# Cross-attention in a decoder block: K, V and maxima units dealt evenly over twelve key steps, and the value product cut 112 + 112

## The chip, the cores and the metric

The kernel runs on one core of a Trainium2 chip. The metric is the device time of one execution in microseconds (us); the times shown are medians over runs.

## The reference

One decoder layer with post-norm, batch 32, 56 queries of width 128, and a context of 1500 rows of width 128 for each batch:

```
x = LN(x + linear_attention(x))                        # 16 heads of 8, 32 features
q = x @ Wq.T + bq;  k = ctx @ Wk.T + bk;  v = ctx @ Wv.T + bv
a = softmax(q k / sqrt(8)) v     per head              # 56 x 1500 scores, 16 heads
x = LN(x + a @ Wo.T + bo)
h = x @ W1 + b1
x = LN(x + relu(h + c1 * sin(theta + 0.1 h)) @ W2 + b2)
```

The cross-attention (second line to fourth) is most of the work and all of what the change touches.

## The kernel before, in words

The front part computes the linear attention for all batches and the queries of the cross-attention. Then comes one `body(b)` for each of the 32 batches, on each engine in its own written order: bodies 0 and 1, a loop over pairs of bodies, and bodies 30 and 31. A body has twelve key steps t of 125 context rows. The last part is the feed-forward network.

In a step TensorE makes the scores of all heads (`score`, L831, four matmuls of 224 columns, in two alternating pairs of PSUM banks), ScalarE takes their exponential (`exp`, L576), and TensorE multiplies the exponentials of the step before by the values (`pv`, L846 and L851) into bank 7, `O`. The value product has for each of four head groups one matmul over three of the group's four heads (168 columns, 32 weights: a block of ones for the denominators and the values) and one over the fourth (56 columns, 16 weights). They are fp32, and each leaves two records.

Between these, TensorE works on the batches that follow, in units. Each unit fills one of the three ring banks (banks 4 to 6), in turn:

- K (three a batch, L794): a third of the key projection, nine fp16 matmuls of 500 columns for three units, for batch b + 2. ScalarE rounds the result to fp16 (`k_hi`, L594, `kh`), and VectorE then writes the remainder (`k_lo`, L1091, `kl`), after which the bank is free.
- V (three a batch, L800): twelve matmuls of 128 columns for batch b + 1; ScalarE copies them to `v_ext` (L581).
- M (21 a batch, L807): scores over 500 keys whose maximum VectorE takes (`m_max`, L1098). After the 21st, `m_row` folds them, X (L811) transposes them, ScalarE copies that to `mT` and SyncE places it as row 96 of `q_diag`, so that the scores come out reduced by a bound on the maximum.
- R (L814, L815): spreads the denominators of batch b - 1; VectorE inverts them (L1112, `r_sb`) and scales O with them (L1116).
- Y (L820, in bodies of even b): the output projection of the pair of batches before.

Before a unit starts, TensorE waits until the unit that last held the bank is done (`held`, `DONE`). `unit_plan` places them: R at step 0, V after steps 0, 2 and 4, two or three M in each of steps 1 to 9, Y at step 6, X at step 11, and the three K units after step 11, with the last value product among them. VectorE takes the results in the same order; after the first K it copies O out of its bank (`o_copy`, L1126), which the next batch's first value product waits for.

`kh` and `kl` have one buffer each. SyncE copies them to `k_stack` by twelve transfers a batch (L355, two of three parts from `kh`). GpSimd splits the context into two fp16 halves (`split`, L442, L444) and makes the masked queries `q_diag` and `q_max`.

## Time and profile before

| | |
|---|---|
| median of 3 runs | 889.09 us (886.41 to 890.37) |
| the profiled execution, its time | 889.02 us |
| its span | 887.2 us |
| TensorE busy | 825.6 us, 93% of the span |
| VectorE busy | 692.8 us, 78% |
| ScalarE busy | 559.0 us, 63% |
| GpSimd busy | 294.3 us, 33% |
| mean granted TensorE clock | 0.974 |

The busy shares are of the whole span. A group of instructions is given by its line, engine and operation with its count and mean duration. The loop over the pairs fills most of the span; in the timeline a row is a run of like instructions, with the start of the first and the time they cover, and the distance between the starts of two rows is what the first really took. In the forty slices each digit is a share in tenths. A released wait is shown in brackets behind the row that had to wait.

### The profile page before, as it was taken

To read this page: it belongs to the slowest core of one execution; us is meant where nothing else is said; L and a number is where in the kernel's file an instruction comes from. 1 tells how busy PE (TensorE), PEld (TensorE's weight loads), DVE (VectorE), ACT (ScalarE), POOL (GpSimd) and SP (SyncE) were. 2 spreads that over 40 slices of the span, in tenths; PEclk is the share of its full clock that TensorE was granted. 3 is DMA by queue.
4 is the path that set the end of the run, shared out by engine and by line. 5 is a ranking of instruction groups with operands and counts; after the bars stand their busy time and mean duration, and the time that the engine had idled before them with its cause. 6 is when DMAs were issued, how large, how long until landed. Compare 5 with 4: busy or idle time off the path is not lost.

```text
span 887.2 us, 28853 instructions
## 1 busy us (share of the span) xinstructions
PE 825.6 (93%) x11074; PEld 534.8 (60%) x11074; DVE 692.8 (78%) x1245; ACT 559.0 (63%) x759; POOL 294.3 (33%) x170
## 2 busy tenths in 40 slices
PE   6788669999999999999999999999999999998884
PEld 3555426666666666666666666666666666666553
DVE  7767687778787878787878787878787878788498
ACT  4566517666666666666666666666666666666863
POOL 6010524333333333333333333333333333300263
PEclk9989959999999999999999999999999999999898
DMA  6000044333333333333333333333333332222001
GB/s 201 1 10 21 21 129 105 92 86 90 86 87 87 86 88 87 87 86 88 85 87 88 86 86 88 87 87 89 85 92 82 93 84 78 52 53 55 1 1 42
DMA packets 29864, 67.37 MB, mean 76 GB/s; under 512 B 8072, under 2 KB 13192, under 8 KB 29704
## 3 DMA queue, kind: packets, MB, share of 16 engines
q1 hardware_dynamic: 29832, 66.94, 28.7%
q8 instruction: 21, 0.34, 0.2%
q14 instruction: 11, 0.09, 0.0%
HBM read 27.50 MB, written 0.92 MB: 32 GB/s over the span
## 4 chain that ended last, share of the span: by engine, by line
PE 73%; DVE 15%; ACT 5%; issue 5%; DMA 1%; DVEq 0%; POOL 0%; ACTq 0%
PE psum L807 19%; PE psum L846 16%; PE psum L831 14%; PE psum L800 6%; PE psum L794 6%; DVE r_sb L1112 5%; PE psum L851 4%; ACT kh L594 2%; PE psum L722 2%; DVE kl L1091 2%; PE psum L820 2%; PE psum L708 1%; DVE k_stack L1226 1%; DVE rden L1025 1%; DVE mx L1098 1%
## 5 line engine op out<-in xcount | busy, mean ns | idle before, releaser
L1098 DVE TENSOR_REDUCE mx<-psum 128x1 f32<-128x500 f32 x672 | 413.0, 672 | 52.7 <-PE psum L807 49.5
L576 ACT ACTIVATE probs<-psum 125x896 f32<-125x896 f32 x384 | 352.7, 919 | 149.9 <-PE psum L831 146.4
L807 PE MATMUL psum<-kh,q_max 128*128 128x500 f16 x672 | 234.5, 383 | 7.3 <-DVE mx L1098 2.0
L831 PE MATMUL psum<-q_diag,k_stack 97*128 97x224 f16 x1536 | 212.9, 261 | 2.7 <-DMA q_diag<-mT 1.8
L846 PE MATMUL psum<-probs,v_ext 125*32 125x168 f32 x3072 | 189.3, 319 | 1.2 <-ACT probs L576 1.2
L831 PEld LDWEIGHTS psum<-q_diag,k_stack 97*128 97x128 f16 x1536 | 140.7, 98 | 46.6 <-issue 16.9
L442 POOL CAST c_hl<-c_in 128x1500 f16<-128x1500 f32 x32 | 45.9, 1434 | 267.8 <-PE psum L800 261.9
L1091 DVE SCALAR_TENSOR_TENSOR kl<-psum,pack,kh 128x500 f16<-128x500 f32 x96 | 68.0, 735 | 83.4 <-ACT kh L594 83.4
L846 PEld LDWEIGHTS psum<-probs,v_ext 125*32 125x32 f32 x3072 | 60.6, 108 | 114.9 <-issue 97.2
L450 POOL TENSOR_TENSOR q_diag<-q_stack,pack 96x896 f16<-96x896 f32 (+1 forms) x32 | 54.2, 1693 | 171.0 <-PE psum L831 158.7
L851 PE MATMUL psum<-probs,v_ext 125*16 125x56 f32 x3072 | 108.4, 213 | 0.0
L851 PEld LDWEIGHTS psum<-probs,v_ext 125*16 125x16 f32 x3072 | 90.0, 97 | 14.9
L444 POOL TENSOR_TENSOR c_hl<-c_in,c_hl 128x1500 f16<-128x1500 f32 x32 | 97.1, 3034 | 2.6
L581 ACT COPY v_ext<-psum 125x512 f32<-125x512 f32 x96 | 56.3, 586 | 60.2 <-PE psum L800 60.0
L807 PEld LDWEIGHTS psum<-kh,q_max 128*128 128x128 f16 x672 | 65.2, 97 | 47.8 <-DVE mx L1098 18.1
L594 ACT ACTIVATE kh<-psum,pack 128x500 f16<-128x500 f32 x96 | 63.6, 677 | 28.7 <-PE psum L794 28.7
L800 PE MATMUL psum<-WvH,c_hl 128*128 128x128 f16 x768 | 75.7, 221 | 0.0
L800 PE MATMUL psum<-WvL,c_hl 128*128 128x128 f16 x384 | 69.4, 219 | 0.0
L800 PEld LDWEIGHTS psum<-WvH,c_hl 128*128 128x128 f16 x768 | 55.8, 98 | 6.7
L794 PE MATMUL psum<-c_hl,WkH 128*128 128x500 f16 x192 | 58.6, 388 | 0.0
L459 POOL TENSOR_TENSOR q_max<-qh,pack 128x896 f16<-128x896 f32 (+1 forms) x32 | 54.0, 1688 | 0.0
L1112 DVE RECIPROCAL r_sb<-psum 128x224 f32<-128x224 f32 x32 | 49.5, 1547 | 0.2 <-PE psum L815 0.2
(143 smaller groups left out, 735.0 us busy)
## 6 DMA issues: line engine op xcount, KB each, us to landing
c_in<-ctx_in SPq DMA_DIRECT2D x32, 750.0 KB, 4.3
k_stack<-kh SPq DMA_DIRECT2D x256, 93.8 KB, 2.2
k_stack<-kl SPq DMA_DIRECT2D x128, 93.8 KB, 2.2
pack<-pack_in SPq DMA_DIRECT2D x1, 1107.0 KB, 5.9
q_stack<-qh SPq DMA_DIRECT2D x32, 32.0 KB, 1.8
out<-x_all SPq DMA_DIRECT2D x8, 112.0 KB
pack<-pack_in SPq DMA_DIRECT2D x1, 848.5 KB, 4.7
x_all<-x_in SPq DMA_DIRECT2D x2, 336.0 KB
```

Source lines behind the costliest of these rows:

```text
L444: nc.gpsimd.tensor_tensor(c_hl[:, buf, 1, 0:S], c_in[:, buf, :], c_hl[:, buf, 0, 0:S], ALU.subtract).then_inc(c_split, 1)
L576: nc.scalar.activation(probs[0:KP, t % PBUF, :].rearrange("p (a c) -> p a c", a=2), scores[t % 2][0:KP, :, 0:2 * GC], ACT.Exp, scale=SCALE ...
L594: nc.scalar.activation(kh[:, i * CH:(i + 1) * CH], bank[:, 0:CH], ACT.Identity, bias=w("bk")).then_inc(kh_done, 1)
L794: last = nc.tensor.matmul(bank[:, 0:CH], wt[:, :], c_hl[:, u, part, i * CH:(i + 1) * CH], start=(k == 0), stop=(k == 2))
L800: last = nc.tensor.matmul(bank[:, j * P:(j + 1) * P], c_hl[:, u, part, at:at + P], wt[:, :], start=(k == 0), stop=(k == 2))
L807: last = nc.tensor.matmul(bank[:, 0:CH], q_max[u][:, r * P:(r + 1) * P], kh[:, c * CH:(c + 1) * CH], start=True, stop=True)
L831: last = nc.tensor.matmul(scores[t % 2][:, g // 2, (g % 2) * GC:(g % 2 + 1) * GC], k_stack[u][0:ROWS, g, t * KP:t * KP + P], q_diag[u][0:R ...
L846: nc.tensor.matmul(O[32 * j:32 * j + 32, 0:3 * N], v_ext[u][0:KP, t, j, 0:32], probs[0:KP, t % PBUF, at:at + 3 * N], start=(t == 0), stop= ...
L851: last = nc.tensor.matmul(O[32 * j:32 * j + 16, 3 * N:GC], v_ext[u][0:KP, t, j, 32:48], probs[0:KP, t % PBUF, at + 3 * N:at + GC], start=F ...
L1091: dve.scalar_tensor_tensor(kl[:, i * CH:(i + 1) * CH], bank[:, 0:CH], w("bk"), kh[:, i * CH:(i + 1) * CH], ALU.add, ALU.subtract).then_inc ...
L1098: dve.tensor_reduce(mx[:, i:i + 1], bank[:, 0:CH], AX.X, ALU.max).then_inc(mx_done, 1)
L1112: dve.reciprocal(r_sb[:, u, :], bank[:, 0:GC]).then_inc(r_inv, 1)
```

## The change

The units are dealt anew over the twelve steps. Each step has two parts, one ahead of the value product and one behind it (`PLAN`):

- V stays behind steps 0, 2 and 4. K moves from the end of the body to behind steps 6, 8 and 10. R moves from step 0 to step 3, Y from 6 to 7, X from 11 to 9.
- Of the 21 maxima of a batch seven (`M2`) are made one body earlier, in steps 8 to 11, and fourteen (`M1`) in steps 0 to 7: two ahead of the value product in most steps, one behind it in every fourth. Their order goes by thirds of K, so that the first seven need the first K unit only. The first body makes all 21 for batch 1, and the seven early ones for batch 2.
- Where a step begins with a pair of maxima, TensorE waits for both banks before the first of them.
- VectorE makes `kl` of a K unit not when its turn comes but behind the next maximum (`split_late`).
- The last value product of a batch moves into step 0 of the next, behind its pair of maxima, and `o_copy` with it.
- `kh` and `kl` have two buffers; SyncE has one more wait, for the stack before.
- The value product and R are cut into 112 + 112 columns, both with 32 weights; the selector and the output weights are laid out to suit.
- The scratch for dynamic DMAs in SBUF is set to 1024 bytes; GpSimd starts none.

```diff
@@ -99,37 +99,59 @@
 PROJECT_LAG = 5
 AHEAD = 2
 ROOT_UNIT = 4
-M_COUNTS = (2, 2, 3, 2, 3, 2, 3, 2, 2)
-V_STEPS, Y_STEP = (0, 2, 4), 6
-X_STEP = 11
-TAIL = [("K", c) for c in range(KC)]
-
-
-def unit_plan(u):
-
-    steps = [[] for _ in range(KT)]
-    m = 0
-    for t, count in enumerate(M_COUNTS, start=1):
-        for _ in range(count):
-            steps[t].append(("M", m))
-            m += 1
-    for i, t in enumerate(V_STEPS):
-        steps[t].append(("V", i))
-    steps[X_STEP].append(("X", 0))
-    steps[0].insert(0, ("R", 0))
-    if u == 0:
-        steps[Y_STEP].insert(0, ("Y", 0))
+EARLY_M = 7
+U1_SHIFT = 0
+M_ORDER = [(r, c) for c in range(KC) for r in (0, 4, 1, 5, 2, 6, 3)]
+SHARED = MB // 2
+PLAN = ((("M1", "M1"), ("V",)), (("M1", "M1"), ()), (("M1", "M1"), ("V",)), ((), ("M1", "R")),
+        (("M1", "M1"), ("V",)), (("M1", "M1"), ()), (("M1", "M1"), ("K",)), ((), ("M1", "Y")),
+        (("M2", "M2"), ("K",)), (("M2", "M2"), ("X",)), (("M2", "M2"), ("K",)), ((), ("M2",)))
+FIRST = {(0, 1): 2, (1, 1): 1, (2, 1): 2, (3, 0): 2}
+
+
+def unit_plan(u, first=False):
+
+    made = {"M1": 0 if first else EARLY_M}
+    steps = []
+    for t, parts in enumerate(PLAN):
+        step = []
+        for part in range(2):
+            kinds = list(parts[part])
+            if first:
+                kinds += ["M1"] * FIRST.get((t, part), 0)
+            units = []
+            for kind in kinds:
+                if kind == "Y" and u:
+                    continue
+                units.append((kind, made.get(kind, 0)))
+                made[kind] = made.get(kind, 0) + 1
+            step.append(units)
+        steps.append(step)
+    assert made["M1"] == NM and made["M2"] == EARLY_M and made["V"] == made["K"] == KC
     return steps
...
@@ -254,7 +276,8 @@
         c_in = sb("c_in", [P, 2, S])
         c_hl = sb("c_hl", [P, 2, 2, S + 4], F16)
-        kh, kl = sb("kh", [P, S], F16), sb("kl", [P, S], F16)
+        kh = [sb(f"kh{i}", [P, S], F16) for i in range(2)]
+        kl = [sb(f"kl{i}", [P, S], F16) for i in range(2)]
         k_stack = [sb(f"k_stack{i}", [P, G, S + 4], F16) for i in range(2)]
         q_diag = [sb(f"q_diag{i}", [P, HQ], F16) for i in range(2)]
...
@@ -350,7 +373,9 @@
                     sp.wait_ge(kl_done, (n + 1) * KC)
                     settle(sp, sp_settled)
-                    for c, part in enumerate((kh, kh, kl)):
+                    wait_past(sp, k_stacked, n * 192)
+                    settle(sp, sp_settled)
+                    for c, part in enumerate((kh[u], kh[u], kl[u])):
                         for g in range(G):
                             sp.dma_start(k_stack[u][32 * c:32 * c + 32, g, 0:S],
...
@@ -782,11 +807,15 @@
                 front(QUADS - 1, True, False)
-                def unit(kind, i, n, u, bank, before):
+                def release(before):
                     if before is not None:
                         held, j, k = before
                         pe.wait_ge(DONE[held], k * PER[held] + j + 1)
+
+                def unit(kind, i, n, u, bank, before):
+
+                    release(before)
                     if kind == "K":
                         if i == 0:
...
+                    elif kind in ("M1", "M2"):
+                        r, c = M_ORDER[i]
+                        if i % MB == 0:
+                            pe.wait_ge(kh_done, n * KC + c + 1)
                         if i == 0:
-                            pe.wait_ge(kh_done, n * KC + KC)
                             pe.wait_ge(qm_ready, n + 1)
                         last = nc.tensor.matmul(bank[:, 0:CH], q_max[u][:, r * P:(r + 1) * P],
-                                                kh[:, c * CH:(c + 1) * CH], start=True, stop=True)
+                                                kh[u][:, c * CH:(c + 1) * CH], start=True, stop=True)
                     elif kind == "X":
                         pe.wait_ge(m_cast, n + 1)
                         last = nc.tensor.transpose(bank.bitcast(F16)[0:MB, 0:P], m16[:, :], ident16[:, :])
                     elif kind == "R":
...
@@ -843,29 +873,32 @@
                     pe.wait_ge(p_ready, b * KT + t + 1)
                     for j in range(G):
                         at = j * GC
-                        nc.tensor.matmul(O[32 * j:32 * j + 32, 0:3 * N], v_ext[u][0:KP, t, j, 0:32],
-                                         probs[0:KP, t % PBUF, at:at + 3 * N], start=(t == 0), stop=(t == KT - 1),
+                        nc.tensor.matmul(O[32 * j:32 * j + 32, 0:2 * N], v_ext[u][0:KP, t, j, 0:32],
+                                         probs[0:KP, t % PBUF, at:at + 2 * N], start=(t == 0), stop=(t == KT - 1),
                                          skip_group_check=True)
                     for j in range(G):
                         at = j * GC
-                        last = nc.tensor.matmul(O[32 * j:32 * j + 16, 3 * N:GC], v_ext[u][0:KP, t, j, 32:48],
-                                                probs[0:KP, t % PBUF, at + 3 * N:at + GC], start=False,
+                        last = nc.tensor.matmul(O[32 * j:32 * j + 32, 2 * N:GC], v_ext[u][0:KP, t, j, 16:48],
+                                                probs[0:KP, t % PBUF, at + 2 * N:at + GC], start=False,
                                                 stop=(t == KT - 1), skip_group_check=True)
                     last.then_inc(pv_done, 1)
-                def body(b, pair, u, s1, s2, before):
-
-
-                    held = [("X", 0, b)] * RING
-                    for c in range(KC):
-                        if s2:
-                            held[slots[1 - u]["K", c]] = ("K", c, b + 1)
-
-                    def go(kind, i):
-                        n = {"K": b + 2, "R": b - 1, "Y": pair - 1}.get(kind, b + 1)
-                        if {"K": s1, "R": before, "Y": before}.get(kind, s2):
-                            slot = slots[u][kind, i]
-                            unit(kind, i, n, u if kind == "K" else 1 - u, ring[slot], held[slot])
+                def of_batch(kind, b, pair):
+                    return {"K": b + 2, "M2": b + 2, "R": b - 1, "Y": pair - 1}.get(kind, b + 1)
+
+                def body(b, pair, u, s1, s2, before, held):
+
+                    first = not before
+                    held = dict(held)
+
+                    def go(units):
+                        units = [unit for unit in units if active(unit[0], s1, s2, before)]
+                        paired = len(units) > 1 and units[0][0] in ("M1", "M2") and units[0][1] % MB in (0, 2, 4)
+                        for k, (kind, i) in enumerate(units):
+                            n, slot = of_batch(kind, b, pair), slots[u, first][kind, i]
+                            if k == 0 and paired:
+                                release(held[slots[u, first][units[1]]])
+                            unit(kind, i, n, u if kind in ("K", "M2") else 1 - u, ring[slot], held[slot])
                             held[slot] = (kind, i, n)
...
@@ -873,17 +906,20 @@
                         score(b, t, u)
                         if not s2 and t in X2T_STEPS:
                             x2_T(X2T_STEPS.index(t))
-                        half = (len(plans[u][t]) + 1) // 2
-                        for kind, i in plans[u][t][:half]:
-                            go(kind, i)
+                        go(plans[u, first][t][0])
+                        if t == 0 and before:
+                            pv(b - 1, KT - 1, 1 - u)
                         if t >= lag:
                             pv(b, t - lag, u)
-                        for kind, i in plans[u][t][half:]:
-                            go(kind, i)
-                    for c in range(KC):
-                        go("K", c)
-                        if c < lag:
-                            pv(b, KT - lag + c, u)
+                        go(plans[u, first][t][1])
+                    if not s2:
+                        for t in range(KT - lag, KT):
+                            pv(b, t, u)
+
...
-                def k_lo(n, i, bank):
+                def k_lo(n, i, u, bank):
                     dve.wait_ge(kh_done, n * 3 + i + 1)
                     if i == 0:
-                        wait_past(dve, k_stacked, n * 192)
-                    dve.scalar_tensor_tensor(kl[:, i * CH:(i + 1) * CH], bank[:, 0:CH], w("bk"),
-                                             kh[:, i * CH:(i + 1) * CH], ALU.add, ALU.subtract).then_inc(kl_done, 1)
+                        wait_past(dve, k_stacked, (n - 1) * 192)
+                    dve.scalar_tensor_tensor(kl[u][:, i * CH:(i + 1) * CH], bank[:, 0:CH], w("bk"),
...
+                    first = not before
+                    late = []
+
+                    def split_late():
+                        while late:
+                            i = late.pop()
+                            k_lo(b + 2, i, u, ring[slots[u, first]["K", i]])
+
                     for t in range(KT):
-                        for kind, i in plans[u][t]:
-                            if kind in "MRY":
-                                bank = ring[slots[u][kind, i]]
-                            if kind == "M" and s2:
-                                m_max(b + 1, i, bank)
-                                if i == NM - 1:
-                                    m_row(b + 1)
-                                    if not s1:
-                                        dve.wait_ge(y_added, 4 * LAST)
-                                        stats_of(0, early)
-                                        variances(0, early, 1)
-                            if kind == "R" and before:
-                                invert(b - 1, 1 - u, bank)
-                                scale_o(b - 1, 1 - u)
-                            if kind == "Y" and before:
-                                add_y(pair - 1, bank)
-                    for i in range(KC):
-                        if s1:
-                            k_lo(b + 2, i, ring[slots[u]["K", i]])
-                        if i == 0:
-                            o_copy(b, u)
+                        for part in range(2):
+                            for kind, i in plans[u, first][t][part]:
+                                bank = ring[slots[u, first][kind, i]]
+                                if kind == "M1" and s2:
+                                    m_max(b + 1, i, bank)
+                                    split_late()
+                                    if i == NM - 1:
+                                        m_row(b + 1)
+                                        if not s1:
+                                            dve.wait_ge(y_added, 4 * LAST)
+                                            stats_of(0, early)
+                                            variances(0, early, 1)
+                                if kind == "M2" and s1:
+                                    m_max(b + 2, i, bank)
+                                    split_late()
+                                if kind == "R" and before:
+                                    invert(b - 1, 1 - u, bank)
+                                    scale_o(b - 1, 1 - u)
+                                if kind == "Y" and before:
+                                    add_y(pair - 1, bank)
+                                if kind == "K" and s1:
+                                    late.append(i)
+                            if t == 0 and part == 0 and before and s2:
+                                o_copy(b - 1, 1 - u)
                 for b in range(2):
...
@@ -1287,10 +1339,10 @@
         t[name + "T"][:] = f["L0_xattn_" + name].T
     for h in range(H):
         j, s = divmod(h, 4)
-        at = 32 * j + (8 + 8 * s if s < 3 else 0)
+        at = 32 * j + (8 + 8 * (s % 2))
         t["WoSlots"][at:at + HD, s * P:(s + 1) * P] = f["L0_xattn_Wo"].T[h * HD:(h + 1) * HD]
     t["selA"][32 * (part // 32), part] = 1
-    t["selB"][32 * (part // 32) + 8, part] = 1
```

## Rows read from the trace of the kernel before

**Rows 1.** Page, busy table and forty slices: TensorE and its granted clock.
```profile
PE 825.6 (93%) x11074; PEld 534.8 (60%) x11074; DVE 692.8 (78%) x1245; ACT 559.0 (63%) x759; POOL 294.3 (33%) x170
...
PEclk9989959999999999999999999999999999999898
```

**Rows 2.** Windows view: busy us (instructions) by engine, clock, DMA share, GB/s.
```profile
170.00:760.00 590.00, 585.02 (x8396) 379.08 (x8396) 466.76 (x786) 388.64 (x508) 206.36 (x106) 1.00 0.33 86
```

**Rows 3.** Chain of waits, whole span: start, us, what.
```profile
178.50 1.56 DVE r_sb L1112
...
798.44 1.56 DVE r_sb L1112
```

**Rows 4.** Timeline, step of the loop, TensorE: start, us, instructions.
```profile
301.54 0.49 PE L846 MATMUL psum<-probs,v_ext 125*32 125x168 f32 x8
...
301.84 0.28 PE L851 MATMUL psum<-probs,v_ext 125*16 125x56 f32 x8
...
302.06 0.39 PE L807 MATMUL psum<-kh,q_max 128*128 128x500 f16 x1
...
302.28 0.55 PE L831 MATMUL psum<-q_diag,k_stack 97*128 97x224 f16 x4
...
302.67 0.38 PE L807 MATMUL psum<-kh,q_max 128*128 128x500 f16 x1
...
302.97 0.49 PE L846 MATMUL psum<-probs,v_ext 125*32 125x168 f32 x8
```

**Rows 5.** Timeline, end of a batch and start of the next, TensorE.
```profile
307.23 0.60 PE L794 MATMUL psum<-c_hl,WkH 128*128 128x500 f16 x2
...
308.49 0.60 PE L794 MATMUL psum<-c_hl,WkH 128*128 128x500 f16 x2
...
309.13 0.58 PE L794 MATMUL psum<-c_hl,WkH 128*128 128x500 f16 x2
...
309.92 0.56 PE L831 MATMUL psum<-q_diag,k_stack 97*128 97x224 f16 x4
...
310.32 0.46 PE L814 MATMUL psum<-o_sb,pack 128*128 128x168 f32 x2
...
310.84 0.28 PE L800 MATMUL psum<-WvH,c_hl 128*128 128x128 f16 x2
...
311.52 0.55 PE L831 MATMUL psum<-q_diag,k_stack 97*128 97x224 f16 x4
```

**Rows 6.** Chain of waits, one batch: Y.
```profile
321.44 0.91 PE psum L820 x8
```

**Rows 7.** Timeline: an exponential, a maxima matmul and its reduction.
```profile
302.87 0.92 ACT L576 ACTIVATE probs<-psum 125x896 f32<-125x896 f32 x1 [0.73 <-PE psum L831]
...
304.93 0.39 PE L807 MATMUL psum<-kh,q_max 128*128 128x500 f16 x1
...
305.35 0.68 DVE L1098 TENSOR_REDUCE mx<-psum 128x1 f32<-128x500 f32 x1 [0.16 <-PE psum L807]
```

**Rows 8.** Timeline: VectorE around K and R, and TensorE's wait.
```profile
309.03 0.74 DVE L1091 SCALAR_TENSOR_TENSOR kl<-psum,pack,kh 128x500 f16<-128x500 f32 x1 [2.58 <-ACT kh L594]
...
311.35 1.55 DVE L1112 RECIPROCAL r_sb<-psum 128x224 f32<-128x224 f32 x1
...
312.95 0.10 PEld L807 LDWEIGHTS psum<-kh,q_max 128*128 128x128 f16 x1 [0.31 <-DVE r_sb L1112]
...
313.24 2.43 DVE L1098 TENSOR_REDUCE mx<-psum 128x1 f32<-128x500 f32 x4
```

**Rows 9.** Page, groups: the value product (busy, mean ns, idle before).
```profile
L846 PE MATMUL psum<-probs,v_ext 125*32 125x168 f32 x3072 | 189.3, 319 | 1.2 <-ACT probs L576 1.2
...
L851 PE MATMUL psum<-probs,v_ext 125*16 125x56 f32 x3072 | 108.4, 213 | 0.0
```

**Rows 10.** Timeline: SyncE issues the first eight stack transfers.
```profile
311.52 5.00 SPq L355 DMA_DIRECT2D k_stack<-kh  x8
```

**Rows 11.** Timeline, TensorE ahead of the loop.
```profile
111.81 1.44 PE L745 MATMUL psum<-pack,aT 128*128 128x128 f32 x5 [3.97 <-DVE aT L1027]
```

More of the change, by code:

```diff
@@ L125, in ring_slots, with active @@
+def active(kind, s1, s2, before):
+    return {"K": s1, "M2": s1, "R": before, "Y": before}.get(kind, s2)
 def ring_slots():
[L127 to L132 removed]
+    rounds = {}
+    for u, first in ((0, False), (1, False), (0, True)):
+        rounds[u, first] = [unit for step in unit_plan(u, first) for part in step for unit in part]
+    return {key: {unit: (k + key[0] * U1_SHIFT) % RING for k, unit in enumerate(units)}
+            for key, units in rounds.items()}
@@ L135, in early_bank, with left_in_ring @@
+def left_in_ring(slots, u, first, s1, s2, before):
+    left = {}
+    for (kind, i), slot in slots[u, first].items():
+        if active(kind, s1, s2, before):
+            left[slot] = (kind, i)
+    return left
 def early_bank(kind, i):
@@ L630, in body @@
                                 x2_T(X2T_STEPS.index(t))
-                    if s1:
-                        for i in range(3):
-                            k_hi(b + 2, i, ring[slots[u]["K", i]])
                 def root_f(k, lo, hi, count):
```

85 lines of the change are left out of this document (45 added, 40 removed).

## The prediction

> **What bounds the kernel now.** I read the page first: the busy table gives TensorE 93% of the span, and in the forty slices its granted clock is 0.9 or more but for two early ones [rows 1]. The windows view of the cross-attention loop then gives 585.0 us of TensorE in 590 [rows 2]: nothing else is near (VectorE 467, ScalarE 389, GpSimd 206), and the clock is 1.00, the 2.4 GHz level. But a modelled matmul ends late, so "busy" hides short waits, and the start times have to be read. The chain of waits gives the period: the long reciprocal L1112 comes up at 178.50 and at 798.44, 14 pairs of batches apart [rows 3], so a pair takes 44.28 us and a batch 22.14.
>
> The timeline gives every part of that period as a distance between starts [rows 4, 5]. Score group 0.39 us (302.28 to 302.67). Maxima matmul 0.21. Value product: 0.52 from its first matmul to the next unit (301.54 to 302.06), and 0.09 in front of it, because the maxima matmul at 302.67 is followed by it only 0.30 later; 0.61 together. K unit 0.63 (308.49 to 309.13). V unit 0.68 (310.84 to 311.52). R 0.52 (310.32 to 310.84). Y 0.91 [rows 6], every other batch. X, 128 columns where a maxima matmul has 500, about 0.05. Twelve scores, 21 maxima, three K, three V, twelve value products, R, X and half a Y are 4.68 + 4.41 + 1.89 + 2.04 + 7.32 + 0.52 + 0.05 + 0.46 = 21.37 us. The other 0.77 us of the period is waiting. So this kernel is TensorE's issue order plus 3% of waits, and a change of order is judged by the waits that it makes.
>
> **What a wait costs here.** Three PSUM banks form a ring: each unit needs the bank of the unit three places before it. A maxima matmul is followed 0.42 us after its start by its reduction (304.93, 305.35) [rows 7]. Four reductions in a row take 2.43 us and a single one 0.68 (305.35) [rows 7, 8], so they follow each other every 0.59; I take 0.60, and 0.67 for the last. TensorE has the bank 0.05 later: the reciprocal of R starts at 311.35 and lasts 1.55, and TensorE's next weights load is at 312.95, after a wait of 0.31 that is the present price of that unit [rows 8]. VectorE's next reduction is at 313.24, 0.34 after the reciprocal, with the scaling of O between. Of a K unit VectorE makes kl after ScalarE's kh, in 0.74 (309.03) [rows 8].
>
> **The change, part by part.** I walk the new order in distances between starts.
>
> *Value product 112 + 112.* The records of L846 last 319 ns and those of L851 213 [rows 9]: 106 ns for 112 columns, so 56 columns are some 0.05 us a pass. The first group loses 56 columns in both its passes: 0.09 to 0.10 saved. The second gains them, but its eight records lie within 0.28 us, so their starts spread over 0.07 [rows 4], more than the streaming of two such short passes would need; part of the added columns fits into that, and I put the loss at 0.07. I take 0.59 for the product instead of 0.61, some 0.28 us a batch; bounds 0 and 0.05 a product. The same for R: 0.45 instead of 0.52.
>
> *New TensorE work* is then 4.68 + 4.41 + 1.89 + 2.04 + 7.08 + 0.45 + 0.05 = 20.60 us without Y and 21.51 with it. With no waits at all the mean would be 21.06.
>
> *K at steps 6, 8 and 10.* VectorE's split of a K unit now stands behind the next maximum (split_late), and only then is K's bank free. Three places:
> (a) K at step 10, maximum at step 11, then step 0 of the next batch, whose pair of maxima needs K's bank (the pair waits for both of its banks). From the step-11 maximum to the pair: 0.42 + 0.60 + 0.74 + 0.05 = 1.81 us, where TensorE has only 0.21 + 0.39 of work. Wait 1.21.
> (b) K at step 6, maximum at 7, pair at 8: again 1.81. Without Y there is 0.60 of work, wait 1.21; with Y 1.51, wait 0.30.
> (c) K at step 8, pair of maxima at step 9, then X in K's bank: 1.81 from the first maximum, work 0.42 + 0.59, wait 0.80. The second maximum's reduction stands behind the split, so its bank is free at 0.42 + 0.60 + 0.68 + 0.67 + 0.05 = 2.42 (the split 0.68 when more follows), and the pair of step 10 is due at 1.81 + 0.05 + 0.39: another 0.17.
> In the kernel before, K, K, K, R stood together: K's bank was asked for 3.09 us after K's start (307.23, 310.32), later than the 2.54 at which its kl had ended (309.03 + 0.74) [rows 5, 8].
>
> *R at step 3.* From the maximum before it to r_inv: 0.42 + 0.60 + 1.55 + 0.05 = 2.62. V at step 4 needs R's bank; the work up to it is 0.21 + 0.45 + 0.39 + 0.42 + 0.59 = 2.06. Wait 0.56. VectorE then scales (0.34), reduces both maxima of step 4, and frees the second at 2.57 + 0.34 + 0.60 + 0.67 + 0.05 = 4.23; the pair of step 5 is due at 2.62 + 0.68 + 0.39 = 3.69. Wait 0.54.
>
> *Sum.* Without Y 1.21 + 1.21 + 0.97 + 1.10 = 4.49 us of waits, period 25.09; with Y 3.58, period 25.09. A pair takes 50.2 us against 44.28, 5.9 more. Thirty of the 32 bodies have this form or nearly so: 15 x 5.9 = 89 us.
>
> *What I cost at nothing.* ScalarE: an exponential starts 0.59 us after its scores and lasts 0.92 (302.28, 302.87) [rows 4, 7], so the value product is due 1.56 us after the scores. TensorE now comes to it after 1.44 or more of work plus the waits, which cover ScalarE's K and V copies in between; without that cover a late exponential costs 0.1 to 0.3 us a step. SP: the twelve transfers of the K stack start when the last kl is there, 1.6 us after the first scores now (309.92, 311.52), and the first eight issue in 5.0 us [rows 5, 10], so the stack is there long before the next batch; the added wait for the stack before it is met by then, and behind it stands only the small diagonal row, whose X now comes at step 9 and so earlier. GpSimd's split starts after V as before, and K is due at step 6 of the next batch instead of its end, still more than half a batch later. The shift to partition 24 in the selectors moves nothing.
>
> *Ends.* The first body takes seven more maxima (7 x 0.60 on VectorE, 4.2) less R, its waits and Y; some 2 more. Body 30 loses seven maxima and its K, and its layer statistics run earlier; some 2 less. Sum 0, bounds 5 either way.
>
> The profiled execution took 889.02 us, the median of the runs is 889.09. **889 + 89 = 978 us.**
>
> **Rivals.**
> *The waits are there but half as long* (0.08): (a) to (c) partly covered. Half of some 4.0 a batch gives back 60 us: 918; a third, 938. Against it: each term is two reductions or a reduction and a split in one queue, all with rows.
> *The waits do not bind, and the order pays* (0.08), the other side: VectorE would have to be through maximum and split in the 0.60 us that TensorE needs from step 11 to the pair, instead of 1.81. Then the period is 21.06 and 30 x 1.08 = 32 us go: 857. In its favour: the present wait of 0.31 on the reciprocal leaves step 0. It decides where all these waits together fall below 1.08 us a batch; between 0.9 and 1.2 the result would be no change (0.02).
> *The clock falls* (0.04). The granted clock was 0.5 in the slice from 111 to 133 us [rows 1], behind a wait of TensorE of 3.97 us (until 111.81) [rows 11]; in the loop, with a wait of 0.31 in each batch, it stayed at 1.00. The new loop works 20.6 us in 25.1 with no wait over 1.21. A granted mean of 0.9 would add 2.3 us to a batch, 69 us: 1047. The Trainium skill (TensorE: Matmul & The Clock Gate, A second HAM failure mode) says that frequent micro-idles while cycling through PSUM banks made the gate oscillate, which would be this rival; the trace has a ring of that kind at 1.00, but none with waits this long.
> The forecast itself holds 0.78.
>
> **How the numbers follow.** The likeliest case's own range is 955 to 1005: the value product's bounds are -10 and +8, the ends 5, and a tenth or two on each of the six waits some 15. To leave no more than 2 in 10 out, the range reaches down over most of the half-length case and stays above the fast one: 920 to 1010. A change of under 0.5% (4.4 us) could not be told from none. Slower by more: 0.78 + 0.08 + 0.04 = 0.90; same 0.02; faster 0.08.
>
> **What would show it.** In the new profile the pair should take 50.2 us. TensorE should wait for kl three times in a batch without Y, 1.2, 1.2 and 0.8 us, each time with maximum, then split in VectorE's queue; with Y the wait at step 8 should be 0.3. The reciprocal should cost 0.56 and the maxima behind it 0.54. VectorE's share should fall from 0.79 [rows 2] to about 0.70. The value product should take 0.50 start to start. I am wrong if VectorE splits K before the maximum, if the pairs do not wait, or if the clock of the loop leaves 1.00.

## The result, and the profile after

The changed kernel takes 998.90 us (median of 4 runs, 996.67 to 1002.05) where the kernel before takes 887.75 us beside it (885.81 to 890.37): a ratio of 1.125, 95% interval 1.120 to 1.130. It is slower, by the mechanism of the forecast, 978 us, and by 21 us more than that.

The page after: the busy table, the granted clock, and three groups (busy us, mean ns of one, idle time before them and what ended it).

```profile
PE 839.1 (84%) x11074; PEld 512.4 (51%) x11074; DVE 699.0 (70%) x1245; ACT 554.9 (56%) x759; POOL 294.3 (30%) x170
...
PEclk9899799999999999999999999999999999999898
...
L1136 DVE TENSOR_REDUCE mx<-psum 128x1 f32<-128x500 f32 x672 | 429.9, 673 | 240.1 <-PE psum L837 240.0
...
L876 PE MATMUL psum<-probs,v_ext 125*32 125x112 f32 x3072 | 153.8, 272 | 0.0
L881 PE MATMUL psum<-probs,v_ext 125*32 125x112 f32 x3072 | 144.6, 260 | 0.0
```

TensorE has as many instructions as before and fell from 93% to 84% [rows 1]. VectorE fell as well, from 78% to 70%: no engine became the bound, they wait for each other. In the stretch that [rows 2] show:

```profile
170.00:760.00 590.00, 514.71 (x7227) 309.64 (x7223) 407.12 (x678) 330.24 (x436) 178.11 (x91) 1.00 0.28 75
```

514.7 us of TensorE in 590, 87%, where it was 99%; the clock stayed at 1.00, the 2.4 GHz level, so the time is not the clock's. The chain of waits gives the period; the long reciprocal is now L1151, and it is on the chain in every batch:

```profile
294.20 1.48 DVE r_sb L1151
...
319.92 1.47 DVE r_sb L1151
...
345.69 1.47 DVE r_sb L1151
```

From 294.20 to 345.69 is a pair of batches: 51.49 us, where it was 44.28 and 50.2 was forecast. Over 15 pairs the added 7.2 us are 108 of the 111 us.

Where it waits is in the timeline of TensorE. From here on such lines give start, duration, engine, line, instructions and, in brackets, the idle time before and its releaser. The first six lines are the end of a batch and the start of the next, behind the K unit of step 10; the rest are the step with R and the two behind it:

```profile
284.95 0.39 PE L837 MATMUL psum<-kh,q_max 128*128 128x500 f16 x1
285.30 0.55 PE L861 MATMUL psum<-q_diag,k_stack 97*128 97x224 f16 x4
286.83 0.59 PE L837 MATMUL psum<-kh,q_max 128*128 128x500 f16 x2 [0.97 <-DVE kl L1128]
287.35 0.40 PE L876 MATMUL psum<-probs,v_ext 125*32 125x112 f32 x8
287.57 0.38 PE L881 MATMUL psum<-probs,v_ext 125*32 125x112 f32 x8
287.88 0.29 PE L829 MATMUL psum<-WvH,c_hl 128*128 128x128 f16 x2
...
293.10 0.39 PE L837 MATMUL psum<-kh,q_max 128*128 128x500 f16 x1
293.32 0.37 PE L844 MATMUL psum<-o_sb,pack 128*128 128x112 f32 x2
...
293.75 0.55 PE L861 MATMUL psum<-q_diag,k_stack 97*128 97x224 f16 x4
...
295.72 0.28 PE L829 MATMUL psum<-WvH,c_hl 128*128 128x128 f16 x2 [0.35 <-DVE r_sb L1151]
...
297.39 0.38 PE L837 MATMUL psum<-kh,q_max 128*128 128x500 f16 x1 [0.45 <-DVE mx L1136]
```

And VectorE's queue under it:

```profile
285.37 0.68 DVE L1136 TENSOR_REDUCE mx<-psum 128x1 f32<-128x500 f32 x1 [1.43 <-PE psum L837]
285.96 0.73 DVE L1128 SCALAR_TENSOR_TENSOR kl<-psum,pack,kh 128x500 f16<-128x500 f32 x1
...
287.25 1.26 DVE L1136 TENSOR_REDUCE mx<-psum 128x1 f32<-128x500 f32 x2 [0.55 <-PE psum L837]
...
294.12 1.55 DVE L1151 RECIPROCAL r_sb<-psum 128x224 f32<-128x224 f32 x1
```

The maximum at 284.95 is reduced from 285.37, the split starts at 285.96 and ends at 286.69, and the pair that needs K's bank starts at 286.83: 1.88 us from the maximum. TensorE had only the maximum itself and one score group for that time. VectorE had been idle for 1.43 us before the reduction: both engines wait, in turn. The maximum before R is at 293.10, the unit in R's bank at 295.72 (2.62 later), the pair behind it at 297.39 (4.29). One list of waits for the whole stretch (us in total, times, longest) names the three releasers:

```profile
PE psum L837 <- DVE kl L1128: 40.2, 35, 1.2
PE psum L841 <- DVE kl L1128: 15.8, 23, 0.7
PE psum L837 <- DVE mx L1136: 9.8, 22, 0.4
PE psum L829 <- DVE r_sb L1151: 8.0, 23, 0.3
```

The split of K alone has 56 of 74 us. (The brackets begin only where a modelled matmul has ended, some 0.2 us after the next could have started, so distances between starts are what to add up.)

### The profile page after: what moved, and what is told of

It reads as the page before. It is cut to its first block, busy times and chain, and to the rows that moved or that the text cites. A ratio compares the mean times of both kernels' runs of the same rounds, so it can differ in the third digit from the quotient of the medians.

```text
span 995.5 us, 28992 instructions
## 1 busy us (share of the span) xinstructions
PE 839.1 (84%) x11074; PEld 512.4 (51%) x11074; DVE 699.0 (70%) x1245; ACT 554.9 (56%) x759; POOL 294.3 (30%) x170
## 4 chain that ended last, share of the span: by engine, by line
PE 62%; DVE 25%; issue 8%; ACT 2%; DVEq 1%; DMA 0%; POOL 0%; ACTq 0%
PE psum L837 15%; PE psum L861 11%; PE psum L876 11%; DVE mx L1136 8%; PE psum L823 7%; DVE kl L1128 7%; PE psum L881 6%; PE psum L829 5%; DVE r_sb L1151 5%; PE psum L747 2%; PE psum L733 1%; PE psum L841 1%; DVE k_stack L1277 1%; DVE rden L1062 1%; DVE stats_f L1196 1%
## 5 line engine op out<-in xcount | busy, mean ns | idle before, releaser
L1136 DVE TENSOR_REDUCE mx<-psum 128x1 f32<-128x500 f32 x672 | 429.9, 673 | 240.1 <-PE psum L837 240.0
L837 PE MATMUL psum<-kh,q_max 128*128 128x500 f16 x672 | 208.2, 380 | 70.6 <-DVE kl L1128 49.6
L861 PEld LDWEIGHTS psum<-q_diag,k_stack 97*128 97x128 f16 x1536 | 136.7, 98 | 46.4 <-issue 17.2
L876 PE MATMUL psum<-probs,v_ext 125*32 125x112 f32 x3072 | 153.8, 272 | 0.0
L881 PE MATMUL psum<-probs,v_ext 125*32 125x112 f32 x3072 | 144.6, 260 | 0.0
L876 PEld LDWEIGHTS psum<-probs,v_ext 125*32 125x32 f32 x3072 | 60.8, 108 | 134.0 <-issue 130.5
L837 PEld LDWEIGHTS psum<-kh,q_max 128*128 128x128 f16 x672 | 53.4, 98 | 126.1 <-DVE mx L1136 83.6
L881 PEld LDWEIGHTS psum<-probs,v_ext 125*32 125x32 f32 x3072 | 87.2, 111 | 0.0
L1151 DVE RECIPROCAL r_sb<-psum 128x224 f32<-128x224 f32 x32 | 49.5, 1547 | 1.1 <-PE psum L845 1.1
```

Source lines behind the costliest of these rows:

```text
L837: last = nc.tensor.matmul(bank[:, 0:CH], q_max[u][:, r * P:(r + 1) * P], kh[u][:, c * CH:(c + 1) * CH], start=True, stop=True)
L861: last = nc.tensor.matmul(scores[t % 2][:, g // 2, (g % 2) * GC:(g % 2 + 1) * GC], k_stack[u][0:ROWS, g, t * KP:t * KP + P], q_diag[u][0:R ...
L876: nc.tensor.matmul(O[32 * j:32 * j + 32, 0:2 * N], v_ext[u][0:KP, t, j, 0:32], probs[0:KP, t % PBUF, at:at + 2 * N], start=(t == 0), stop= ...
L881: last = nc.tensor.matmul(O[32 * j:32 * j + 32, 2 * N:GC], v_ext[u][0:KP, t, j, 16:48], probs[0:KP, t % PBUF, at + 2 * N:at + GC], start=F ...
L1136: dve.tensor_reduce(mx[:, r * KC + c:r * KC + c + 1], bank[:, 0:CH], AX.X, ALU.max).then_inc(mx_done, 1)
L1151: dve.reciprocal(r_sb[:, u, :], bank[:, 0:GC]).then_inc(r_inv, 1)
```

## The experiments

In the changed kernel three things differ at once that the waits could come from: K's split stands behind the next maximum, a pair of maxima waits for both of its banks before it starts, and the order of the units is another. The first two are undone alone and together; the order is replaced by two others. The "theory" below is the walk of distances of the prediction; times are medians, with the ratio to the kernel before in the same session (887.75 to 890).

**1. The split of K in its turn.** (e1_split_in_turn)

```
-                                    late.append(i)
+                                    k_lo(b + 2, i, u, bank)
```

> The changed kernel, but VectorE makes kl of a K unit in its turn instead of behind the next maximum. Theory (TensorE waits for K's bank, which is freed by maximum, then split): K's bank is free some 2.4 us after K's start instead of 3.4, so the waits of about 1.2 us before the pairs at steps 0 and 8 shrink to about 0.2, while the pair at step 9 is reduced later and the next pair waits some 0.6 more. Sum by the walk of distances: 2.4 us less per pair of batches than the changed kernel's 51.5, about 49.0, 37 us less in all: 960. Rival (the wait comes from ScalarE's kh or from the number of units between, not from the order in VectorE's queue): within 5 us of 998.

967.31 us, ratio 1.087 (1.085 to 1.090), 7 us over the theory: 31.6 us come back, over a quarter of what was lost. The waits for kl shrink and others take their place, for the maxima:

```profile
PE psum L837 <- DVE mx L1136: 30.8, 60, 0.7
PE psum L829 <- DVE r_sb L1151: 8.4, 24, 0.3
PE psum L837 <- DVE kl L1128: 4.0, 11, 0.4
PE psum L841 <- DVE kl L1128: 2.5, 12, 0.2
```

The maximum now stands behind the split in VectorE's queue, and the pairs wait for it instead.

**2. No wait ahead for pairs.** (e2_no_pair_wait)

```
-                            if k == 0 and paired:
-                                release(held[slots[u, first][units[1]]])
```

> The changed kernel without the wait of a pair's first maximum for the second one's bank. Theory: where the second bank is the late one (step 0 of odd bodies, step 8 without Y, steps 4 and 5) the first maximum of 0.21 us runs in front of the wait, so 0.1 to 0.2 us come back at each such place, about 1.0 us per pair of batches, 15 us in all: 983. Rival (the pair wait is what costs the 100 us): back to within 20 us of 888.

977.90 us, ratio 1.100 (1.097 to 1.103): 21 us, where the theory had 15.

**3. Both undone, the new order kept.** (e7_in_turn_no_pair)

> e1 and e2 together: kl in its turn, and no pair wait. e1 gave 31 us and e2 20 us over the changed kernel. Theory: they work on the same waits from two sides, so that the K waits at steps 0 and 8 nearly vanish (0.2 us of the first maximum covers what is left); by the walk 3.8 us less a pair, 47.7, 941 in all. Rival (independent, additive): 31 + 20 less, 947; or the smaller alone, 967.

931.52 us, ratio 1.048 (1.046 to 1.051): 67.4 us, more than the 52.6 of the two by themselves and than the theory's 58. That each rule undone alone leaves the other's wait to end last would explain it; it is read from the lists of waits, not tested by itself. What is left is 43 us over the kernel before, and number 11 shows that it goes with the order.

**4. K's bank free early.** (e3_k_bank_free_at_kh) The split reads kh, in SBUF, not the bank, and K's bank counts as free at kh. The fp16 remainder of K is left out by this.

```
-        DONE = {"K": kl_done, ...
+        DONE = {"K": kh_done, ...
-                    dve.scalar_tensor_tensor(kl[u][:, i * CH:(i + 1) * CH], bank[:, 0:CH], w("bk"),
+                    dve.scalar_tensor_tensor(kl[u][:, i * CH:(i + 1) * CH], kh[u][:, i * CH:(i + 1) * CH], w("bk"),
```

> The changed kernel, but kl is made from kh instead of from K's PSUM bank, so the bank is free once ScalarE has made kh (1.53 us after K's start, before the next use in every place); the split stays behind the maximum with the same cost to VectorE. This leaves out the fp16 remainder of K, so scores are less exact. Theory: the waits on kl at steps 0, 8 and 9 go (4.1 us a pair of batches in steps 0 and 8, 1.6 at X), but VectorE's queue is as long as before and the maxima behind the split are late: 0.3 us more at step 1, 0.7 at step 9 and 0.8 at step 10. By the walk 2.3 us less per pair, about 49.2, 963 in all. Rival A (the K bank alone): 5.7 us less a pair, 912. Rival B (the K bank is not the wait): 998.

1026.07 us, ratio 1.153 (1.150 to 1.156), slower than the changed kernel and 63 us over the theory. The miss has a reason of its own, in its timeline at the start of a batch:

```profile
316.44 1.70 POOL L475 TENSOR_TENSOR q_diag<-q_stack,pack 96x896 f16<-96x896 f32 x1 [8.69 <-PE psum L861]
...
317.66 2.66 DVE L1128 SCALAR_TENSOR_TENSOR kl<-kh,pack 128x500 f16<-128x500 f16 x1
...
318.10 1.69 POOL L484 TENSOR_TENSOR q_max<-qh,pack 128x896 f16<-128x896 f32 x1
```

An instruction that took 0.73 us with the same operands elsewhere in this run (at 308.91, GpSimd idle) took 2.66 while GpSimd ran two of 1.7 us. In the changed kernel the same split, with the bank as its source, stands in the same place beside the same two GpSimd instructions and takes 0.73:

```profile
284.76 1.69 POOL L475 TENSOR_TENSOR q_diag<-q_stack,pack 96x896 f16<-96x896 f32 x1 [9.15 <-PE psum L861]
...
285.96 0.73 DVE L1128 SCALAR_TENSOR_TENSOR kl<-psum,pack,kh 128x500 f16<-128x500 f32 x1
...
286.42 1.69 POOL L484 TENSOR_TENSOR q_max<-qh,pack 128x896 f16<-128x896 f32 x1
```

The slow one ends at 320.32, 0.53 after GpSimd's second instruction (318.10 + 1.69). The Trainium skill (SBUF — State Buffer, Who interferes with whom) says that a VectorE instruction with two SBUF inputs contends with a GpSimd instruction that reads SBUF, and that the one that comes second is blocked for the whole of the other; the trace agrees that they contend, with 2.66 us against 0.73. It does not agree on the order: the split started at 317.66, before GpSimd's second instruction, and still ended after it.

The slow split is most of the miss: two batches at a granted clock of 1.00 took 52.48 us (reciprocal to reciprocal, 300.57 to 353.05) where 49.2 were expected, 49 us over 15 pairs. The rest is of the size of the clock's share: its mean over 170 to 760 us was 0.98, and some batches had 0.94 and took 27.86 us (353.05 to 380.91) instead of some 26.2. The experiment changed the operand's memory together with the wait, and so says nothing on the wait. Number 5 asks the same without that, though it also takes the split's work from VectorE.

**5. No split at all, and 6. the split done twice.** (e6_no_split, e5_split_twice) In number 5 kl is zero (the remainder of K is left out), VectorE has no split, and K's bank is free at kh. In number 6 VectorE makes each split twice, the first into a spare tile, and waits for it.

```
+                    dve.scalar_tensor_tensor(kl_spare[:, 0:CH], bank[:, 0:CH], w("bk"),
+                                             kh[u][:, i * CH:(i + 1) * CH], ALU.add, ALU.subtract).then_inc(spare_done, 1)
+                    dve.wait_ge(spare_done, n * 3 + i + 1)
```

> The changed kernel without the split's work: kl stays zero (the fp16 remainder of K is left out), VectorE only passes the semaphore on, and K's bank is free once ScalarE has made kh. It replaces e3, where the split from SBUF took 2.66 us in one place of each batch beside GpSimd. Theory: the waits on K go entirely; the waits around R (0.45 + 0.54) and some 0.2 each at steps 1, 4, 10 stay. By the walk of distances 4.7 us less per pair than the changed kernel's 51.5: 46.8, 928 in all. Rival (K's waits merely cover a wait behind them that would then show): over 960.

930.63 us, ratio 1.048 (1.045 to 1.050), as the theory has it (928): 68 of the 111 us are the split's, by its work, its place in the queue and its hold on the bank together.

> The changed kernel with the split of each K unit done twice by VectorE (once into a spare tile, then as before): one suspected cost doubled, 0.74 us and some 0.05 for the semaphore between. VectorE is busy 0.70 of the span, so the 96 x 0.79 = 76 us would fit into its idle time. Theory (each split stands between a maximum and TensorE's next use of the bank): every one of the six waits per pair of batches grows by the whole 0.79, 4.7 us a pair, 71 us in all: 1068. Rival (VectorE's order is not on the path): under 1010.

1120.52 us (2 runs, 1114 to 1127), ratio 1.261 (1.251 to 1.270): in the direction of the theory, and 52 us over its number. Its stretch of the loop:

```profile
170.00:760.00 590.00, 481.97 (x6244) 288.08 (x6243) 395.55 (x643) 287.55 (x377) 153.11 (x79) 0.93 0.24 64
```

The mean clock is 0.93 here, where the changed kernel has 1.00, so part of the time was spent at 1.2 GHz. The trace lets the two causes be told apart, batch by batch (from reciprocal to reciprocal):

```profile
264.21:292.22 28.01, 22.85 (x321) 13.99 (x319) 20.07 (x34) 14.43 (x19) 7.81 (x4) 1.00 0.23 62
292.22:322.77 30.55, 25.15 (x313) 14.47 (x311) 19.97 (x33) 14.55 (x19) 7.81 (x4) 0.89 0.26 69
```

The two behind them took 29.61 us at 0.94 and 31.28 at 0.89, and then the four come again. The batch with the full clock has 28.01 us. The changed kernel's has 25.75, and with three splits more the theory makes that 25.75 + 3 x 0.79 = 28.1. Thirty such batches add 30 x 2.26 = 68 us to the changed kernel, 1067. The mean of the four is 29.86, 1.85 more, and 30 x 1.85 = 56 us is the size of what was missing: it is all in the batches with the lower clock. Before the clock fell TensorE had waited 2.02 and 1.46 us (until 362.49 and 367.11); a score group of 0.55 us then took 0.95 (370.35).

**7. R's bank read by nobody.** (e11_r_bank_unread) The reciprocal takes O's copy in SBUF, and the bank counts as free at R's product (the spreading of the denominators is left out).

> The changed kernel, in which the reciprocal reads O's copy in SBUF instead of R's product in the bank (left out: the spreading of the denominators over the rows), so that R's bank counts as free when its product is done. If the bank of R is what the step after R waits for (R to V at step 4, 0.5 us a batch), that wait goes: 999 - 15 = 984. If VectorE's queue behind the 1.55 us reciprocal is what counts (the reductions after it free their banks as late as before), the wait only moves to the next pair, and the time stays at 995 to 1000.

999.60 us, ratio 1.124 (1.122 to 1.126): no change. TensorE's timeline there:

```profile
295.60 0.39 PE L837 MATMUL psum<-kh,q_max 128*128 128x500 f16 x1
...
299.90 0.59 PE L837 MATMUL psum<-kh,q_max 128*128 128x500 f16 x2 [0.86 <-DVE mx L1136]
```

And VectorE's under it:

```profile
296.62 1.54 DVE L1151 RECIPROCAL r_sb<-o_sb 128x224 f32<-128x224 f32 x1
298.20 0.39 DVE L1155 TENSOR_TENSOR o_n<-o_sb,r_sb 128x224 f32<-128x224 f32 x1
298.51 1.26 DVE L1136 TENSOR_REDUCE mx<-psum 128x1 f32<-128x500 f32 x2
```

The wait of 0.35 for the reciprocal is gone and the next one is 0.86 where it was 0.45; from the maximum before R to the second pair are 4.30 us, as before the edit (4.29). Two waits in a row with one cause: VectorE is occupied for 1.9 us, and the last wait behind it gets what the first gives up. The list of waits says the same for the whole stretch: no r_sb, and 19.6 us for the maxima, where the changed kernel has 8.0 and 9.8.

**8. The kernel before with 112 + 112 columns alone** (e4_before_112; value product and R).

> The kernel before with only the value product and R cut into 112 + 112 columns (and the selector and output weights to suit). Prediction on record: value product 0.59 instead of 0.61, R 0.07 less, together 0.35 us a batch and 11 us less. What the changed kernel's trace shows: first group 0.21 to 0.22, second 0.31 to the next unit, 0.52 in all as before, so no gain from the product; R 0.43 instead of 0.52, 0.09 a batch, of which the wait on the reciprocal keeps nothing: 1 to 3 us less, 885. Rival (it costs): over 892.

889.09 us, ratio 0.9988 (0.9976 to 0.9999): a gain of a tenth of a per cent. In its timeline the first group has become shorter and the second longer by as much:

```profile
300.73 0.40 PE L846 MATMUL psum<-probs,v_ext 125*32 125x112 f32 x8
300.94 0.38 PE L851 MATMUL psum<-probs,v_ext 125*32 125x112 f32 x8
301.25 0.39 PE L807 MATMUL psum<-kh,q_max 128*128 128x500 f16 x1
```

0.52 us from its first matmul to the next unit, as in [rows 4].

**9. Another order, with short units between the late banks** (e8_plan_long_beside_long; split in its turn, no wait ahead for pairs, as in number 3). PLAN gives the two parts of each step; it was chosen by the walk so that no bank that is freed late is asked for early.

```
+PLAN = ((("M1",), ("M1", "M1")), ((), ("M1", "V", "M1")), (("R", "M1"), ()), (("V", "M1"), ()),
+        (("M1", "M1", "K"), ("M1",)), (("Y", "V", "M1"), ("M1",)), ((), ("M1", "M1", "K")), (("M2",), ()),
+        (("M2",), ("M2",)), (("M2", "M2"), ()), (("M2", "K", "X"), ("M2",)), ((), ()))
```

> The changed kernel, kl in its turn and no pair wait as e7, and the units dealt by another rule: M1 in ones and twos through steps 0 to 6, K behind steps 4, 6 and within 10, V at steps 1, 3 and 5, R at step 2, Y at 5, M2 over steps 7 to 10, such that at each reuse of a bank TensorE's work between covers 2.4 us for K and for R and 1.2 us for a maximum. Theory: no bank wait is left; the bare distances add up to 42.9 us a pair, and the two traces show 0.8 to 1.0 more per pair than the walk (loop boundary, semaphores in a row): 43.8 against 44.3 before, 880 to 888 in all, within 1% of the kernel before. Rival (dealing K and V between the steps costs by itself, whatever the order): over 900.

927.02 us, ratio 1.043 (1.041 to 1.046): hardly better than number 3. All waits for K's and R's banks are gone, and a new one stands in each batch:

```profile
320.93 0.22 PE L850 MATMUL psum<-ident,m 128*7 128x128 f16 x1
...
323.98 0.56 PE L870 MATMUL psum<-q_diag,k_stack 97*128 97x224 f16 x4 [1.22 <-DMA q_diag<-mT]
```

X stands at step 10 of this order, and the scores of the next batch need what X starts: ScalarE's copy and a transfer into q_diag, 3.05 us from X to the scores. The walk had no term for that, and so forecast 880 to 888.

**10. The same order with X at step 8.** (e9_order_with_x_at_step_8)

```
-        (("M2",), ("M2",)), (("M2", "M2"), ()), (("M2", "K", "X"), ("M2",)), ((), ()))
+        (("X", "M2"), ("M2",)), (("M2", "M2"), ()), (("M2", "K"), ("M2",)), ((), ()))
```

> The order of e8_plan_long_beside_long with one unit moved: the transpose X stands at step 8, not step 10 (K splits in their turn and no wait ahead for pairs, as there; nothing is left out). Theory, the time is set by distances alone (bank reuse, and some 3.05 us from X to the next batch's first scores over the diagonal's copy and the transfers behind it): the wait of 1.20 us at each first score goes, some 30 batches by 1.1 to 1.2 us, 927 - 35 = 890, 884 to 898. Rival, dealing the units evenly costs by itself (more work of TensorE, VectorE or the transfers beside it): the waits go, but the time stays at 905 or more. A third: the last reductions are now what X waits for (two steps less for them), and the wait moves to X: 905 to 925, with an idle time at X ended by the cast of the maxima.

901.05 us, ratio 1.014 (1.012 to 1.016), 3 us above the range of the theory. 26 of the 35 us come, and two small waits stay, of which the first is the third case of the expectation:

```profile
310.65 0.22 PE L850 MATMUL psum<-ident,m 128*7 128x128 f16 x1 [0.19 <-DVE m L1153]
311.20 0.39 PE L846 MATMUL psum<-kh,q_max 128*128 128x500 f16 x1 [0.33 <-DVE kl L1135]
```

**11. An order with no wait in the walk** (e10_other_order_r_at_step_3), X's 3.1 us among its terms.

```
+PLAN = ((("M1",), ("M1",)), (("M1", "V", "M1"), ("M1",)), (("M1",), ("M1",)), (("M1", "R"), ()),
+        (("M1", "K"), ("Y", "M1")), ((), ("M1", "K", "V")), (("M1",), ()), (("M1", "M1", "K"), ("V", "M2")),
+        ((), ("M2",)), (("X",), ("M2",)), (("M2", "M2"), ()), (("M2",), ("M2",)))
```

> Another order of the same units (nothing left out; splits in their turn, no wait ahead for pairs): R at step 3, the K units at steps 4, 5 and 7, Y at step 4, X at step 9, no V after step 7, short units between them, chosen so that the last holder of a bank has long been done with where it is freed late (K's split, R's reciprocal). By distances no wait is left: 880 to 892. Rival, dealing costs by itself: 905 or more. Between them, 893 to 904, X at step 9 is a little too late for the diagonal (0.3 to 0.5 us a batch).

871.87 us, ratio 0.981 (0.979 to 0.983): faster than the kernel before by 17 us and than the changed one by 127.

```profile
170.00:760.00 590.00, 590.00 (x8657) 383.51 (x8649) 494.83 (x811) 404.71 (x524) 213.18 (x110) 1.00 0.35 87
```

The list has no wait of TensorE in this stretch, and the first K unit of the even batches gives the period:

```profile
281.72 0.58 PE L832 MATMUL psum<-c_hl,WkH 128*128 128x500 f16 x2
...
324.72 0.58 PE L832 MATMUL psum<-c_hl,WkH 128*128 128x500 f16 x2
```

43.00 us for a pair, 21.50 for a batch. Since a modelled matmul ends late, the distances are the better witness: a score group takes 0.38 to 0.40 us up to the next maximum and a maximum 0.21 to 0.23 up to the next score group all through these 43 us, but for one of 0.35 (309.91 to 310.26). So this is the work of the units in this order, with next to no waits.

All else of the change is still in this kernel: seven maxima made a body early, two buffers for `kh` and `kl`, the last value product in the next batch's step 0, 112 + 112 columns. None of these can be what cost the 111 us.

**12. That order with the changed kernel's two rules** (e12_other_order_old_rules), which completes the square.

> The changed kernel with the order of e10_other_order_r_at_step_3 alone: K's split stands behind the next maximum and the pairs wait for both banks, as in the changed kernel (nothing left out). It completes the square: 999 (both as changed), 931.5 (rules alone undone), 871.9 (order too). Theory, distances in both queues: with the splits late again, each of the three K units makes the step behind it wait, 0.6 to 0.75 us at steps 5, 7 and 8, some 1.6 to 2.1 us a batch; the pair rule costs 0 here, since no bank of its pairs is late. 872 + 30 x 1.6 to 2.1 = 920 to 935. Rival, the order heals all and late splits are covered: 872 to 885. Rival, the late splits cost here what they cost in the changed kernel (about 2.2 us a batch with the pairs): 940 or more.

922.19 us, ratio 1.038 (1.035 to 1.042). It is in the range of the theory. Its list of waits holds the split alone:

```profile
PE psum L846 <- DVE kl L1137: 31.5, 64, 0.6
PE psum L832 <- DVE kl L1137: 2.5, 13, 0.2
```

| us | split late, pairs wait | in its turn, no pair wait |
|---|---|---|
| the change's order | 998.9 | 931.5 |
| the other order | 922.2 | 871.9 |

The order is worth 77 or 60 us, the rules 67 or 50.

## Why the prediction was right, and where it was short

*That it is slower, and by what.* Shown. A pair takes 51.49 us and its work, by number 11, 43.00, which leaves 8.5 us for waits. The changed kernel's own rows, where each distance is taken against the same distance without a wait, give 8.2; the prediction had 8.07. Its six places are where the trace has them, each with its own releaser; the smallest, at step 10, is 0.12 where 0.17 was forecast.

*(a) and (b), the split behind a maximum.* From the maximum to the pair 1.81 us were forecast. At step 0 it was 1.88 at 284.95 and 2.02 in the other batch (310.54 to 312.56, though kl ended at 312.29); at step 8 it was 1.80 with Y (301.52 to 303.32) and 1.99 without (327.24 to 329.23). Between the split's end and TensorE's start lay 0.05 to 0.27 us where 0.05 was taken; why it is not the same everywhere is open. With Y the wait at step 8 is 0.30, as forecast (its score group takes 0.69 instead of 0.39). *(c)* X came 1.79 us after its maximum (305.40 to 307.19), forecast 1.81, and the pair behind it 2.45 (307.85), forecast 2.42.

*R at step 3.* 2.62 to the unit in R's bank, forecast 2.62; 4.29 to the pair, forecast 4.23. Number 7 shows what the two terms are: not a bank's wait and a queue's wait, but one occupation of VectorE. Their sum was right. Taking the first away gives nothing; the second was not taken away alone.

*The value product*, the term that was mis-sized. It was put at 0.59 for 0.61, from the reading that the second group's starts were spread over more than its streaming needed, so that part of the added columns would fit in. They did not: the first group gives up 0.08 to 0.09 us and the second takes it back. The trace has 0.52 or 0.53 (287.35 to 287.88), and 0.09 ahead of it again, so 12 x 0.02 = 0.24 us a batch were missing, 7 us in all; number 8 shows the same with nothing else changed. The upper bound given for it, 8 us, holds it. R did fall, to 0.43 (293.32 to 293.75), forecast 0.45.

*The rest of the work.* 21.50 measured against 21.06 forecast. Beside the product's 0.24 a batch it is the score group at one turn in a pair, 0.35 us behind a maximum where 0.21 was taken (284.95 to 285.30), and in number 11 Y, 1.00 where [rows 6] have 0.91. In the changed kernel Y took 0.89 (301.74 to 302.63), but X 0.15 (307.19 to 307.34) where 0.05 was taken. Of the 21 us that were missing, 15 pairs x (43.00 - 42.11) are 13 for work and 15 x (8.5 - 8.07) are 6 for waits; with the 8.2 of the changed kernel's own rows it is 17 and 3. Either way most of it is work that was put too low.

*What was costed at nothing.* ScalarE, SyncE and the transfers show no wait of TensorE in the list, so they were hidden. The prediction gave the waits as their cover; number 11 has next to none, and no matmul in its list waits for them either (weight loads wait for an exponential, up to 0.4 us, and the distances between the matmuls stay as they are). X was hidden too, at step 9; number 9 shows that it ceases to be at step 10.

*The rivals.* Half-length waits: no, 8.2 to 8.5 against 8.07 (and the 918 given for them lay just under the range that was meant to hold most of them). Waits that do not bind: not in this kernel. The 857 us given for it without waits can be held against number 11, which has another order and no waits and takes 872; the difference is again the work of 0.44 us a batch (30 x 0.44 = 13). The falling clock: 1.00 here. Waits of up to 1.2 us, six in a batch, did not bring it down; numbers 4 and 6, with waits of up to 2.1 and 2.0, have means of 0.98 and 0.93. The Trainium skill (TensorE: Matmul & The Clock Gate, A second HAM failure mode) says that frequent micro-idles while PSUM banks are cycled can make the gate oscillate: the changed kernel's trace does not show it; number 6 has a clock that falls and comes back (1.00, 0.89, 0.94 and 0.89 in four batches), and loses some 54 us by it.

## What to carry to other kernels

When units share a ring of banks, write down for every unit the distance from its start to the end of its last reader in that reader's queue, and put at least that much of the main engine's work between the unit and the next taker of its bank; here one walk of that kind over starts gave 978 for a bad order and, once it had a term for X that it first lacked (number 9), found one that takes 872. Evenness by itself decides nothing: the same units, dealt over the same twelve steps, gave 999 and 922 with the two rules, and 932 and 872 without them. A wait that vanishes when it is taken away alone, as R's did, may come back whole at the next one, so test waits by the time, not by their row.

## What the runs showed of the hardware

A VectorE instruction with all its operands in SBUF took 2.66 us beside two GpSimd instructions where it takes 0.73 otherwise; with its main operand in PSUM it took 0.73 beside the same two (number 4). This was not foreseen in the expectation. The four value-product matmuls of a group, on four column tiles and with two records each, took 0.22 us with 112 columns each (287.35 to 287.57), and both groups together took 0.52 us, whether the columns were split 168 and 56 [rows 4] or 112 and 112 (number 8). The granted clock of the loop stayed at 1.00 with waits of TensorE of up to 1.2 us, and had a mean of 0.98 with waits of up to 2.1 (number 4) and 0.93 with waits of up to 2.0 (number 6). In number 6 a batch took 28.01 us at 1.00, and 29.6 to 31.3 us at 0.89 to 0.94.
